# Rearranging the last image and the expert tiles of a hybrid conv-attention-MoE kernel

## The chip, the cores and the metric

The kernel runs on one core of a Trainium2 chip. The metric is the device time in microseconds of one execution, as the median of a few runs. A profile is one execution taken by the hardware profiler; its span goes from the first to the last instruction.

## The reference

Four images of 128 channels x 1024 positions pass through three blocks. (1) Attention over positions: `q, k` of 16 channels, `v` of 128, softmax over 1024 keys, `gamma * out + x`. (2) A linear attention without softmax over the tokens of `_ln_t(t)`: eight heads, whose scores reduce to one factor per head; then `@ proj_w + proj_b`, added to `t`. (3) A mixture of eight experts on `_ln_t(t)`, top 2 of 8:

```python
probs = softmax(flat @ router_w.T); topk_probs, topk_idx = top_k(probs, 2)
topk_probs = topk_probs / (sum(topk_probs) + 1e-09)
gates = einsum('nk,nke->ne', topk_probs, one_hot(topk_idx, 8))
h = silu(einsum('nc,ehc->neh', flat, w1)) * einsum('nc,ehc->neh', flat, w3)
out = einsum('ne,nec->nc', gates, einsum('neh,ech->nec', h, w2))   # t + out is returned
```

Each expert has 341 hidden channels. All is float32.

## The kernel before, in words

The program is a `Block` with one instruction stream per engine, written out by hand: SyncE (`sp`), TensorE (`pe`), ScalarE (`act`), VectorE (`dve`), GpSimd (`pool`). An engine runs its stream in order; semaphores join the streams. So the order of the calls in `image()` and in the tile loops is the schedule.

*Images.* For each of the four images the streams run `image(i)`: softmax attention (`weigh_values`), layer norm, then eight heads in turn (`head_values`: six matmuls of 512 columns; ScalarE keeps the high part in `keep_head_values`, L774; VectorE the low part in `low_head_values`, L960), each pair followed by `project_heads`. Beside it stand the scores of the next image (`beside(n)`: `scores_by_query` and `row_max`) and the routing of the image before: `shift_logits`, `pick_first`, `pick_second`, `keep_ranks` (rank of each token within its expert), `set_slots` (L1061 to L1064: row numbers in the table), and `set_gates` (L1040 to L1047: the two gates). `keep_outT` (L971) adds the bias to a half of the projection, `turn_out` (L507) turns it, `linear_attended` (L977 on) adds it to the token rows and takes statistics, `rstds` on GpSimd (L1323) gives the reciprocal deviation, `norm2` (L932) normalises.

*Row scatters.* GpSimd's `scatter_rows` writes the tokens' normalised rows to `xs_dram`, a table in DRAM with a region per expert: 16 indirect DMAs per image (2 choices x 8 tiles of 128 tokens), each row being 128 values, the result's row number and three spare words (528 bytes). For images 0 to 2 they go out during the next image, 12 ahead of the `rstd` of its second norm and 4 behind it (`SCATTERS_FIRST`).

*Expert tiles.* After the last image come 71 tiles of 128 rows, 41 from rows of images 0 to 2 (`early_table` gives their expert and first row, on one partition of VectorE) and 30 late ones (`late_counts`, `late_table`). For tile t: SyncE gathers 128 rows into one of 8 slots (L337, waits for the result scatter of tile t-8); TensorE turns them (`turn_x`, L622), ScalarE and VectorE split them in a high part (`high_part`, L829) and a low part (`low_part`, L1246); TensorE makes both hidden matrices (`hidden13`, six matmuls into `bank_s`, L372), ScalarE the silu (L824), VectorE the product (`multiply`, L1251); TensorE turns it (L643), VectorE keeps it (`keep_hiddenT`, L1256), TensorE makes the result, ScalarE copies it (`keep_y`, L835), GpSimd scatters it to `y_dram` (L1363). The weights `w13` are split beforehand in two halves (`split_w13`: ScalarE L751, VectorE L1069). The stages of neighbouring tiles overlap.

*Side jobs.* The second half of the last image's rows, its routing, its 16 row scatters (one after each result scatter of tiles 10 to 25) and 8 pad scatters (tiles 26 to 33, `place_pad`: rows of zeros behind each expert's last row) are done between tiles. Tile 41's gather waits for them all.

*Tail.* When all results are scattered, SyncE loads both choices of each of 8 half images (L362), VectorE does gate0 * y0 + t (L1299), ScalarE gate1 * y1 (L865), TensorE adds and turns both by matmuls with the identity, VectorE copies (L1305), SyncE stores (L365).

## Time and profile before

| | us |
|---|---|
| median of 3 runs (549.94 to 553.61) | 552.88 |
| profiled execution, its own time | 552.03 |
| its span | 550.1 |
| TensorE busy in the span | 460.2 (84%) |
| VectorE busy | 316.8 (58%) |
| ScalarE busy | 191.7 (35%) |
| GpSimd busy | 158.7 (29%) |
| mean granted TensorE clock | 0.901 |

Engines in the rows: PE is TensorE's matmuls, PEld its weight loads, DVE VectorE, ACT ScalarE, POOL GpSimd, SP SyncE. "L960" is line 960 of the kernel. A row of the timeline has start and length in us and, in brackets, the engine's idle time before it and what ended it ("remote" is a releaser that the profile doesn't tell). Buffers that share memory carry the name of the first: `probs_sb` is also the gathered rows, results and loads of the tail, `qk_sum_sb` the product, `w_rest_sb` the low part of `w13`.

### The profile page before, as it was taken

The numbers are of one execution on the slowest core, as the hardware profiler recorded it, in microseconds if no ns is written. First come the engines' busy times: TensorE is split into PE (matmuls) and PEld (weight loads), VectorE is DVE, ScalarE is ACT, GpSimd is POOL, SyncE is SP. The second block draws the span as 40 slices with busy tenths as digits, with TensorE's granted clock in tenths as the row PEclk, the third lists the DMA queues.
The fourth block names the chain that finished last, engine by engine and source line by source line (L and its number), as shares of the span: only waits on it lengthen the run. The fifth ranks groups of instructions, "written<-read, shape, count | busy, mean of one in ns | idle before, by whom it ended". The sixth has DMA issues, their size and how long they took to land.

```text
span 550.1 us, 9237 instructions
## 1 busy us (share of the span) xinstructions
PE 460.2 (84%) x2929; PEld 397.3 (72%) x2929; DVE 316.8 (58%) x871; ACT 191.7 (35%) x398; POOL 158.7 (29%) x168
## 2 busy tenths in 40 slices
PE   5879999998889988899875847987778689999847
PEld 3449667887657976578864646987677689999747
DVE  3854687467746569455647734656533345555436
ACT  3060534516217243134133403452222234444343
POOL 1000000100623202504107331335666554444500
PEclk9668999998969989879956986988998989999969
DMA  6800100001100002100001001212222222222187
GB/s 195 281 2 0 39 0 2 1 2 38 41 20 11 12 0 83 45 1 21 1 16 63 15 21 40 55 40 65 64 65 68 63 63 60 69 60 70 41 235 229
DMA packets 28869, 30.21 MB, mean 55 GB/s; under 512 B 5074, under 2 KB 24146, under 8 KB 28696
## 3 DMA queue, kind: packets, MB, share of 16 engines
q1 hardware_dynamic: 24248, 20.09, 13.1%
q0 software_dynamic: 4576, 9.53, 5.1%
q8 instruction: 27, 0.44, 0.3%
q14 instruction: 18, 0.15, 0.1%
HBM read 17.44 MB, written 12.16 MB: 54 GB/s over the span
## 4 chain that ended last, share of the span: by engine, by line
PE 61%; DVE 16%; issue 7%; another core or an unknown queue 5%; ACT 5%; DMA 3%; POOL 1%; SPq 1%; DVEq 0%; POOLq 0%; ACTq 0%
PE bank_c L372 25%; PE bank_s L372 19%; PE bank_a L372 9%; DVE row_max_sb L899 3%; PE bank_c L643 3%; DVE values_sb L960 3%; PE bank_a L622 1%; PE bank_c L443 1%; DVE v_ext_sb L892 1%; DMA probs_sb<-xs_dram 1%; ACT probs_sb L744 1%; DMA y_dram<-probs_sb 1%; DVE ln_sb L932 1%; PE bank_a L507 1%
## 5 line engine op out<-in xcount | busy, mean ns | idle before, releaser
L1363 POOL DMA_INDIRECT y_dram<-probs_sb x71 | 68.0, 957 | 83.8 <-ACT probs_sb L835 80.0
L1331 POOL DMA_INDIRECT xs_dram<-ln2x_sb,slots_sb x64 | 64.7, 1011 | 63.9 <-DVE slots_sb L1064 45.6
L1323 POOL TENSOR_TENSOR rstd_sb<-var_eps_sb,minus_half_sb 128x4 f32<-128x4 f32 x16 | 16.4, 1022 | 195.1 <-DVE var_eps_sb L926 195.1
L774 ACT ACTIVATE values_sb<-bank_s,g_head_sb 128x1024 fp32r<-128x1024 f32 x32 | 35.3, 1113 | 90.9 <-PE bank_s L372 59.7
L372 PE MATMUL bank_c<-v_ext_sb,probs_sb 128*128 128x129 f32 x512 | 62.5, 283 | 4.8 <-issue 3.5
L372 PEld LDWEIGHTS bank_c<-v_ext_sb,probs_sb 128*128 128x128 f32 x512 | 60.9, 198 | 6.7 <-issue 6.7
L372 PE MATMUL bank_c<-values_sb,wp_hi_sb 128*128 128x256 f32 x256 | 59.6, 310 | 0.0
L899 DVE TENSOR_REDUCE row_max_sb<-bank_a 128x1 f32<-128x512 f32 x64 | 41.5, 685 | 27.5 <-remote 14.3
L372 PE MATMUL bank_s<-probs_sb,x_hi_sb 128*128 x142 | 53.4, 376 | 2.9 <-issue 1.4
L372 PEld LDWEIGHTS bank_c<-values_sb,wp_hi_sb 128*128 128x128 f32 x256 | 46.9, 211 | 5.7 <-issue 4.7
L372 PE MATMUL bank_s<-probs_sb,x_lo_sb 128*128 x142 | 47.1, 331 | 0.0
L372 PE MATMUL bank_s<-w_rest_sb,x_hi_sb 128*128 x142 | 47.0, 331 | 0.0
L960 DVE SCALAR_TENSOR_TENSOR values_sb<-bank_s,g_head_sb,values_sb 128x1024 fp32r<-128x1024 f32 x32 | 40.5, 1277 | 7.5 <-ACT values_sb L774 7.4
L1251 DVE TENSOR_TENSOR qk_sum_sb<-probs_sb,bank_s 128x341 f32<-128x341 f32 x36 | 18.4, 512 | 41.8 <-ACT probs_sb L824 29.6
L835 ACT COPY probs_sb<-bank_c 128x128 f32<-128x128 f32 x71 | 18.9, 266 | 63.0 <-PE bank_c L372 35.8
L1256 DVE COPY qk_hi_sb<-bank_c 114x384 f32<-114x384 f32 x71 | 38.9, 548 | 2.9 <-remote 1.5
L1251 DVE TENSOR_TENSOR qk_sum_sb<-v_ext_sb,bank_s 128x341 f32<-128x341 f32 x35 | 17.8, 509 | 38.8 <-ACT v_ext_sb L824 36.9
L643 PE MATMUL bank_c<-cst_s_sb,qk_sum_sb 128*114 128x128 f32 x213 | 36.1, 280 | 3.9 <-DVE qk_hi_sb L1256 3.2
L372 PE MATMUL bank_c<-values_sb,wp_lo_sb 128*128 128x256 f32 x128 | 38.6, 302 | 0.0
L372 PE MATMUL bank_c<-wq_s_sb,qk_hi_sb 114*128 x142 | 29.4, 289 | 10.4 <-ACT probs_sb L835 10.4
L372 PE MATMUL bank_a<-k_stack_sb,q_stack_sb 64*128 64x512 f32 x64 | 31.0, 542 | 8.2 <-DVE row_max_sb L899 3.0
L744 ACT ACTIVATE probs_sb<-bank_s 128x1024 f32<-128x1024 f32 x32 | 32.3, 1024 | 9.2 <-PE bank_s L372 7.6
(189 smaller groups left out, 915.8 us busy)
## 6 DMA issues: line engine op xcount, KB each, us to landing
probs_sb<-xs_dram SPq DMA_DIRECT2D x71, 66.0 KB
probs_sb<-y_dram SPq DMA_DIRECT2D x16, 256.0 KB, 5.2
w_rest_sb<-in_w_dram SPq DMA_DIRECT2D x1, 2728.0 KB, 12.6
xc_sb<-in_x_dram SPq DMA_DIRECT2D x4, 512.0 KB, 3.3
y_dram<-probs_sb POOLq DMA_INDIRECT x71
xs_dram<-ln2x_sb,slots_sb POOLq DMA_INDIRECT x64
xs_dram<-pads_sb SPq DMA_DIRECT2D x1, 528.0 KB, 7.4
wq_s_sb<-in_wq_dram SPq DMA_DIRECT2D x1, 512.0 KB, 3.9
```

The lines of the kernel that those rows point to most:

```text
L372: return nc.tensor.matmul(bank, lhsT, rhs, start=start, stop=stop)
L643: last = nc.tensor.transpose(bank_c[0][0:CHUNK, c * P:(c + 1) * P], hidden[k % 2][:, c * CHUNK:(c + 1) * CHUNK], ident)
L744: nc.scalar.activation(probs[:, m, :], bank_s[m % 2][:, :], ACT.Exp, scale=DQK ** -0.5).then_inc(s.drained, 1)
L774: nc.scalar.activation(vh_hi[:, hd % RING, :], bank_s[hd % 2][:, :], ACT.Copy, scale=g_head[:, hd:hd + 1]).then_inc(vh_high, 1)
L835: nc.scalar.copy(y_rows[k], bank_c[1][:, 0:C]).then_inc(y_kept, 1)
L899: V.reduce_max(row_max2[:, n, h:h + 1], bank_a[h][:, :], AX_X).then_inc(A[h].drained, 1)
L960: V.scalar_tensor_tensor(out=vh_lo[:, hd % RING, :], in0=bank_s[hd % 2][:, :], scalar=g_head[:, hd:hd + 1], in1=vh_hi[:, hd % RING, :].bit ...
L1251: V.tensor_tensor(hidden[k % 2][:, 0:HID], silu1[k % 2], bank_s[k % 2][:, H13 + HID:H13 + HID2], ALU.mult).then_inc(hidden_ready, 1)
L1256: V.tensor_copy(hiddenT[k % 2][0:CHUNK], bank_c[0][0:CHUNK, 0:3 * P].rearrange("p (k n) -> p k n", n=P)).then_inc(hiddenT_ready, 1)
L1323: G.tensor_tensor(rstd[:, tiles], var_eps[:, tiles], minus_half[:, tiles], ALU.pow).then_inc(rstd_ready, 1)
L1331: G.indirect_dma_start(xs_dram, bass.IndirectOffsetOnAxis(ap=slots[:, i, k:k + 1], axis=0), ln2x[:, k // TILES, k % TILES, :], None).then_ ...
L1363: G.indirect_dma_start(y_dram, bass.IndirectOffsetOnAxis(ap=x_rows[k][:, C:C + 1].bitcast(I32), axis=0), y_rows[k], None).then_inc(scatter ...
```

## The change

It rearranges the last image, the tiles and the tail. In all images the gates are made right behind the slots, and travel to the table inside the row (word C+1); the result is scaled by its gate when ScalarE keeps it, and the tail adds only. The order of the results in `y_dram` becomes 8 rows in line for each partition, so the tail's loads take 2048 bytes in line instead of 512.

- *VectorE, image i:* `set_slots(i-1)` and now `set_gates(i-1)` behind low part 0. In the last image both stand ahead of `head_weights`; `early_table` moves from behind low part 0 to behind low part 3; `split_w13(0)` behind `keep_outT(i, 0)`, which itself comes before low parts 6 and 7; then `low_part(0)`, `split_w13(1)`, `low_part(1)`, `linear_attended(i, 0)`, `keep_outT(i, 1)`. `norm2(last, 0)` moves behind tile 0.
- *GpSimd:* all 16 row scatters of image 2 ahead of the `rstd` (they now wait for the gates). Row scatters of the last image from tile 9, behind two tiles of three. The 8 pad scatters go.
- *SyncE:* the pads are 8 plain DMAs, behind the gather of tile 23, from registers with the first row number.
- *TensorE:* `turn_out(last, 0)` behind the seventh head; the first two `turn_x` inside the last projection; routing of the last image at tiles 2, 3 and 6 instead of 4, 5 and 10. In the tail 4 transposes per half instead of 8 matmuls of code.
- *VectorE, tiles:* routing steps packed.

```diff
+    ROWS_FROM = 9
+    PADS_AT = 20
...
+            def place_pads():
+                sp.wait_ge(pads_placed, 1)
+                for e in range(0, EXPERTS, 4):
+                    rows = nc.values_load_multi_w_load_instructions(pad_rows[0:1, e:e + 4], engines=[mybir.EngineType.SP], min_val=0,
+                                                                    max_val=EXPERTS * REGION - P)[1]
+                    for n in range(4):
+                        sp.dma_start(xs_dram[bass.ds(rows[n], P), :], pads[:, e + n, :]).then_inc(pads_stored, 16)
...
+                    if half == 0 and j == PADS_AT:
+                        place_pads()
...
-                    rows = y_dram[k * TOKENS + h * HALF:k * TOKENS + (h + 1) * HALF, :]
-                    sp.dma_start(y_in[:, h, k], rows.rearrange("(n p) c -> p n c", p=P)).then_inc(y_loaded[h], 16)
+                    rows = y_dram[k * TOKENS + h // 2 * N:k * TOKENS + (h // 2 + 1) * N, :].rearrange("(p n) c -> p n c", p=P)
+                    sp.dma_start(y_in[:, h, k], rows[:, h % 2 * 4:h % 2 * 4 + 4, :]).then_inc(y_loaded[h][k], 16)
...
+                if last:
+                    turn_out(i, 0)
...
-                    if k == 1:
+                    if k == 1 and not last:
                         turn_out(i, 0)
+                    if last and k in (4, 7):
+                        turn_x(k // 7, k // 7)
...
-                if t == 4:
+                if t == 2:
                     turn_ln2(final, 1)
-                if t == 5:
+                if t == 3:
                     for h in range(2):
                         route(final, h)
-                if t == 10:
+                if t == 6:
                     rank(final)
...
-                    for k in range(2):
-                        last = mm(bank_a[h % 2][:, j * P:(j + 1) * P], y_in[:, h, k, j, :], ident, start=(k == 0), stop=(k == 1))
+                    last = nc.tensor.transpose(bank_a[h % 2][:, j * P:(j + 1) * P], y_in[:, h, 0, j, :], ident)
...
-                    if i == IMAGES - 1 and hd in (1, 4):
+                    if i == IMAGES - 1 and hd in (3, 5):
                         split_w13(slice(4 * (hd // 4) * HID2, 4 * (hd // 4 + 1) * HID2))
...
-                nc.scalar.copy(y_rows[k], bank_c[1][:, 0:C]).then_inc(y_kept, 1)
+                nc.scalar.activation(y_rows[k], bank_c[1][:, 0:C], ACT.Copy, scale=x_rows[k][:, C + 1:C + 2]).then_inc(y_kept, 1)
...
-                act.wait_ge(y_loaded[h], 32)
-                for j in range(4):
-                    last = nc.scalar.activation(y_in[:, h, 1, j, :], y_in[:, h, 1, j, :], ACT.Copy, scale=gates[:, 1, 4 * h + j:4 * h + j + 1])
-                last.then_inc(y_scaled, 1)
+                act.wait_ge(y_turned, h + 1)
+                nc.scalar.copy(y_out[h], bank_a[h % 2][:, :]).then_inc(out_kept, 1)
...
-                g = [gates[:, k, bass.ds(i * TILES, TILES)] for k in range(2)]
+                g = [ln2x[:, k, :, C + 1] for k in range(2)]
...
                 low_lnT(i)
-                if not last:
+                if last:
+                    set_slots(i - 1)
+                    set_gates(i - 1)
+                    V.memset(hidden[0][:, HID:3 * CHUNK], 0.0)
+                    V.memset(hidden[1][:, HID:3 * CHUNK], 0.0).then_inc(hidden_cleared, 1)
+                else:
                     make_stacks(i + 1)
                 head_weights(i)
...
-                if not first:
+                if not first and not last:
                     set_slots(i - 1)
-                if last:
-                    early_table()
+                    set_gates(i - 1)
...
                 low_head_values(i, 3)
+                keep_bias(i)
                 if last:
-                    split_w13(0)
-                keep_bias(i)
+                    early_table()
...
+                if last:
+                    keep_outT(i, 0)
+                    split_w13(0)
+                else:
                     negate_max(i + 1)
                 low_head_values(i, 6)
+                low_head_values(i, 7)
                 if last:
+                    low_part(0, 0)
                     split_w13(1)
-                low_head_values(i, 7)
-                keep_outT(i, 0)
-                linear_attended(i, 0)
-                if not first and not last:
-                    set_gates(i - 1)
-                keep_outT(i, 1)
-                norm2(i, 0)
+                    low_part(1, 1)
+                    linear_attended(i, 0)
+                    keep_outT(i, 1)
+                else:
+                    keep_outT(i, 0)
+                    linear_attended(i, 0)
+                    keep_outT(i, 1)
+                    norm2(i, 0)
...
                 if t == 0:
+                    norm2(last, 0)
                     linear_attended(last, 1)
-                if t == 2:
+                if t == 1:
                     norm2(last, 1)
+                if t == 3:
+                    shift_logits(last)
                 if t == 4:
-                    set_gates(last - 1)
+                    pick_first(last)
                 if t == 5:
-                    shift_logits(last)
-                if t == 6:
-                    pick_first(last)
-                if t == 8:
                     pick_second(last)
-                if t == 10:
+                if t == 7:
                     keep_ranks(last)
                     place_pads()
+                    set_slots(last)
+                if t == 8:
+                    set_gates(last)
+                if t == 9:
+                    late_counts()
                 if t == 11:
-                    set_slots(last)
-                if t == 13:
-                    late_counts()
-                if t == 15:
                     late_table()
-                if t == 18:
-                    set_gates(last)
...
+            def add_up(h):
+                for k, other in enumerate((t2[:, 4 * h:4 * h + 4, :], y_in[:, h, 1])):
+                    dve.wait_ge(y_loaded[h][k], 16)
+                    V.tensor_tensor(y_in[:, h, 0], y_in[:, h, 0], other, ALU.add).then_inc(y_added, 1)
...
-                if 10 <= t < 26:
-                    scatter_rows(last, range(t - 10, t - 9))
-                if t == 26:
-                    pool.wait_ge(pads_placed, 1)
-                if 26 <= t < 34:
-                    place_pad(t - 26)
+                if ROWS_FROM <= t and (t - ROWS_FROM) % 3 < 2 and (t - ROWS_FROM) // 3 < TILES:
+                    k = (t - ROWS_FROM) // 3 * 2 + (t - ROWS_FROM) % 3
+                    scatter_rows(last, range(k, k + 1))
```

## Rows read from the trace of the kernel before

**Rows 1.** Windows: us, then busy us and count per engine, granted clock, DMA, GB/s.

```profile
core 0: us, PE busy (x) PEld busy (x) DVE busy (x) ACT busy (x) POOL busy (x), PEclk, DMA share, GB/s
...
314.00:334.50 20.50, 7.36 (x43) 6.59 (x42) 8.34 (x23) 1.06 (x3) 4.95 (x5) 0.77 0.10 28
...
386.00:441.00 55.00, 41.07 (x279) 37.22 (x278) 21.94 (x60) 14.45 (x52) 32.83 (x35) 0.97 0.25 65
...
529.70:550.10 20.40, 17.03 (x128) 16.30 (x128) 12.96 (x36) 8.95 (x28) 0.00 (x0) 0.91 0.87 252
```

**Rows 2.** Timeline of VectorE in the last image, 285 to 329 us.

```profile
285.92 0.17 DVE L945 TENSOR_REDUCE qsum_sb<-bank_c 128x8 f32<-128x16 f32 x1 [5.21 <-PE bank_c L372]
...
289.58 0.18 DVE L1064 CAST slots_sb<-small_sb 128x16 int32<-128x16 f32 x1
...
295.99 2.48 DVE L960 SCALAR_TENSOR_TENSOR values_sb<-bank_s,g_head_sb,values_sb 128x1024 fp32r<-128x1024 f32 x2
...
302.64 2.99 DVE L1069 TENSOR_TENSOR w_rest_sb<-w_rest_sb,probs_sb 128x2728 fp32r<-128x2728 f32 x1
...
328.23 0.18 DVE L990 TENSOR_SCALAR ln2x_sb<-tok_sb 128x16 int32<-128x16 int32 x1 [3.27 <-DMA xs_dram<-ln2x_sb,slots_sb]
```

**Rows 3.** Timeline of GpSimd in the last image: first, eleventh and last row scatter.

```profile
290.05 1.03 POOL L1331 DMA_INDIRECT xs_dram<-ln2x_sb,slots_sb  x1 [14.12 <-DVE slots_sb L1064]
...
302.76 3.71 POOL L1331 DMA_INDIRECT xs_dram<-ln2x_sb,slots_sb  x1 [0.30 <-issue]
...
325.94 0.95 POOL L1331 DMA_INDIRECT xs_dram<-ln2x_sb,slots_sb  x1 [0.30 <-issue]
```

**Rows 4.** Timeline of TensorE in the last image, up to the first turned rows.

```profile
297.33 1.22 PE L372 MATMUL bank_s<-lnT_hi_sb,wv_hi_sb 128*128 128x512 f32 x2 [5.61 <-DVE values_sb L960]
...
332.05 0.45 PE L622 MATMUL bank_a<-cst_s_sb,probs_sb 128*128 128x128 f32 x1 [7.82 <-DMA probs_sb<-xs_dram]
```

**Rows 5.** Chain of waits: the six matmuls of tile 0 and of a late tile.

```profile
334.55 2.07 PE bank_s L372 x6
...
514.41 0.94 PE bank_s L372 x6
```

**Rows 6.** Timeline of VectorE: products of tiles 0, 11, 37, 70, and the first gate step.

```profile
337.14 0.51 DVE L1251 TENSOR_TENSOR qk_sum_sb<-probs_sb,bank_s 128x341 f32<-128x341 f32 x1 [2.87 <-ACT probs_sb L824]
...
347.00 0.21 DVE L1040 TENSOR_REDUCE small_sb<-prob_sb 128x8 f32<-128x64 f32 x1
...
367.14 0.51 DVE L1251 TENSOR_TENSOR qk_sum_sb<-v_ext_sb,bank_s 128x341 f32<-128x341 f32 x1 [1.05 <-ACT v_ext_sb L824]
...
447.50 0.51 DVE L1251 TENSOR_TENSOR qk_sum_sb<-v_ext_sb,bank_s 128x341 f32<-128x341 f32 x1 [1.50 <-ACT v_ext_sb L824]
...
517.82 0.51 DVE L1251 TENSOR_TENSOR qk_sum_sb<-probs_sb,bank_s 128x341 f32<-128x341 f32 x1 [0.97 <-ACT probs_sb L824]
```

**Rows 7.** Timeline of GpSimd: two pairs of tiles with extra scatters, and a late tile.

```profile
403.21 0.96 POOL L1363 DMA_INDIRECT y_dram<-probs_sb  x1 [1.60 <-ACT probs_sb L835]
404.47 0.95 POOL L1331 DMA_INDIRECT xs_dram<-ln2x_sb,slots_sb  x1 [0.30 <-issue]
...
409.52 0.95 POOL L1363 DMA_INDIRECT y_dram<-probs_sb  x1 [1.57 <-ACT probs_sb L835]
...
512.94 0.95 POOL L1363 DMA_INDIRECT y_dram<-probs_sb  x1 [1.10 <-ACT probs_sb L835]
```

**Rows 8.** Timeline of VectorE: set-up into image 0, and image 2.

```profile
43.48 0.17 DVE L915 RECIPROCAL rden_sb<-bank_c 128x1 f32<-128x1 f32 x1 [8.78 <-PE bank_c L372]
...
228.63 1.41 DVE L899 TENSOR_REDUCE row_max_sb<-bank_a 128x1 f32<-128x512 f32 x2 [5.72 <-remote]
```

**Rows 9.** DMA view of the tail: GB/s in 40 slices, first 532 to 538 us, then 539 to 543.

```profile
GB/s 307 300 294 297 304 290 280 304 283 290 294 294 280 304 287 280 304 290 280 290 304 280 277 311 280 287 300 287 283 304 287 283 290 300 277 300 297 280 283 307
...
GB/s 297 282 312 261 323 282 313 307 323 369 389 333 338 476 446 369 328 471 430 410 328 430 430 430 328 410 451 451 328 348 512 369 307 225 266 205 123 82 266 389
```

**Rows 10.** The kept result by group, and the tail's timeline: first scaling, last copy.

```profile
L835 ACT COPY probs_sb<-bank_c 128x128 f32<-128x128 f32 x71 | 18.9, 266 | 63.0 <-PE bank_c L372 35.8 <-remote 22.7 <-issue 4.5
...
528.32 1.28 ACT L865 ACTIVATE probs_sb<-probs_sb,gates_sb 128x128 f32<-128x128 f32 x4 [6.42 <-DMA probs_sb<-y_dram]
...
546.95 0.69 DVE L1305 COPY xt_sb<-bank_a 128x512 f32<-128x512 f32 x1 [1.09 <-PE bank_a L372]
```

More of the change, by code:

```diff
@@ L171, in conv_attn_moe_kernel @@
         both = sb("both", [P, TILES, EXPERTS], BF16)
-        gates = sb("gates", [P, 2, IMAGES * TILES])
+        place8 = sb("place8", [P, 1])
         base = sb("base", [P, EXPERTS])
@@ L537, in rank, with turn_x @@
                 last.then_inc(uses.filled, 1)
+            def turn_x(t, k):
+                if t == 0:
+                    pe.wait_ge(A[1].drained, A[1].after(IMAGES - 2, "ln2", 1))
+                at_least(pe, x_lo_ready, t)
+                pe.wait_ge(gathered[k], gathered_value(t, k))
+                nc.tensor.transpose(bank_a[1][:, 0:P], x_rows[k][:, 0:C], ident).then_inc(x_turned, 1)
             def image(i, first=False, last=False):
@@ L785, in copy_ln2, with high_part @@
                 nc.scalar.copy(ln2x[:, 1, 4 * h:4 * h + 4, 0:C], ln2x[:, 0, 4 * h:4 * h + 4, 0:C]).then_inc(ln2_copied, 1)
+            def high_part(t, k):
+                act.wait_ge(x_turned, t + 1)
+                at_least(act, h13_ready, t - 1)
+                nc.scalar.copy(x_hi[k % 2][:], bank_a[1][:, 0:P]).then_inc(x_hi_ready, 1)
             def gate_exps(i):
@@ L852, in _ @@
                     copy_ln2(last, 0)
-                if t == 4:
+                if t == 2:
                     keep_ln2T(last, 1)
                     copy_ln2(last, 1)
-                if t == 8:
+                if t == 5:
                     gate_exps(last)
@@ L1339, in image @@
                     rstds(i, which)
+                early = 2 * TILES if i == IMAGES - 1 else SCATTERS_FIRST
                 if not first:
-                    scatter_rows(i - 1, range(SCATTERS_FIRST))
+                    scatter_rows(i - 1, range(early))
                 rstds(i, 2)
-                if not first:
-                    scatter_rows(i - 1, range(SCATTERS_FIRST, 2 * TILES))
+                if not first and i < IMAGES - 1:
+                    scatter_rows(i - 1, range(early, 2 * TILES))
                 if i < IMAGES - 1:
```

65 lines of the change are left out of this document (18 added, 47 removed).

## Prediction

> **What bounds the kernel now.** I read first the busy time by stretch [rows 1]: after the last image come three stages that wait. From 314 to 334.5 us TensorE is busy 7.36 of 20.5 us; from 386 to 441 it is busy 41.07 of 55, GpSimd 32.83; from 529.7 on the DMA engines are busy 87% of the time. The images before are only brushed by the change.
>
> Then the timelines around the start of the expert tiles [rows 2 to 4]. VectorE waits 5.21 us for the column sums, makes the slots of image 2 at 289.58 and then runs the early table up to 295.99, for which TensorE waits 5.61 us. GpSimd starts the 16 row scatters at 290.05; they follow by 1.26 us each (0.96 and a gap of 0.30); the eleventh takes 3.71. The queue then stops for a reciprocal deviation of the last image, and the last scatter starts at 325.94. VectorE, which waits for them all, goes on at 328.23; TensorE turns the first gathered rows at 332.05, after 7.82 us of waiting, and starts tile 0 at 334.55 [rows 5]. The start hangs on GpSimd's last scatter, not on TensorE.
>
> Then the tiles. The products of tiles 0, 11, 37 and 70 start at 337.14, 367.14, 447.50 and 517.82 [rows 6]. An undisturbed tile takes 2.05 us (scatter 0.95, wait 1.10). Where a row or pad scatter follows each result scatter (24 tiles, 10 to 33), GpSimd issues four in a row, and the next pair of tiles begins 6.31 us later (403.21, 409.52): 3.16 per tile [rows 7]. GpSimd alone would allow 2 x 1.26 = 2.52; the rest is a wait for a result that TensorE hands over late. I see the same lateness in image 2: VectorE stands 5.72 us amid a chain of twelve scatters [rows 8]. In the tail, loads of 512-byte rows run near 290 GB/s; once stores of 2048-byte rows take over, the slices lie around 390 [rows 9]. The 8 halves take 2.4 us each (first scaling 528.32, last copy ends at 547.64 [rows 10]).
>
> **Part by part, in the profiled execution (552.03 us, span 550.1; 0.85 under the median of 552.88).**
>
> *Images 1 and 2: +3.3 us.* The eight gate operations move ahead of the second low part of the heads. They take 1.65 us (the first takes 0.21 [rows 6]; eight such). VectorE is on the path there, so it costs that in each of two images; where they stood, VectorE waits for TensorE afterwards, and nothing comes back. Least 0, if the lateness swallows it; most 3.5. Three small operations added in the set-up lie before VectorE's wait of 8.78 us [rows 8]: 0, uncovered 0.5.
>
> *Start of the tiles: -14 us.* Slots and gates of image 2 go ahead of the head weights, into the 5.21 us wait: 0.95 + 1.65 us from 280.7 on, so scatters start at 283.6. All 16 now stand ahead of the reciprocal deviation: last issue 302.6, landed at 304.8 (325.94 to 328.23 was 2.3). The early table (6.2 us) stands behind the fourth low part. Walking VectorE's new order (low part 1.28, half 0.7): fourth low part done 296.8, table 303.2, fifth and sixth low parts 305.8, out half 306.5, first split 309.5, last two low parts 312.1. The gather needs table and scatters (304.8) and 3.8 us more (328.23 to 332.05 before): 308.6, and the first rows are turned inside the last projection at 312.8. Behind it VectorE has low part 0 (0.3), the second split (2.99), low part 1, the first half's sum and statistics (2.1) and an out half (0.7): first product at 320, 17 us under 337.14. The stretch now runs beside unbroken scatters, as image 2 does; I charge 3 of its 5.72 us: 323. Bounds: -17 (no lateness) and -8 (5.72 and a wait like it again).
>
> The eleventh scatter's 3.71 us begin 0.12 us behind VectorE's split of 2.99 us [rows 2, 3]. The Trainium skill ("SBUF — State Buffer", Who interferes with whom) says that a VectorE operation with two SBUF inputs holds off a GpSimd operation that reads SBUF; the trace agrees. By that rule the split, now at 306.5, meets no scatter; the walk has it so without the rule.
>
> *Tiles 0 to 11: +4 us.* Before: 30.0 us, 7.5 over 11 x 2.05. The same side jobs stay, closer together; slots (0.8), late counts (1.9) and the first half's normalisation (1.1) come in, gates replace gates. 34 us. Bounds 30 and 38 (the late table's 3.3 too).
>
> *Tiles 11 to 32.* Row scatters follow two tiles of three, from 9 to 31; the pads leave GpSimd. Three tiles are five instructions: 5 x 1.26 = 6.3 us, against 6.15 of undisturbed tiles. If the extra 1.27 us (6.31 less 4 x 1.26) is paid once per group, three tiles take 7.6 us, 2.5 each, which I take. Floor 2.1 (GpSimd's pace), ceiling 3.16 (nothing eased). 21 x 2.5 + 2 for the late table = 54.5 us.
>
> Pads on SyncE: two loads of four registers and 8 transfers of 67 KB, ahead of the gather of tile 24. At 290 GB/s they are 1.9 us of DMA; the issues are not shown by rows here, I take 0.5 us each. Gathers run 8 tiles ahead, so this comes to 0; most 3 once.
>
> *Tiles 32 to 70:* 38 x 2.13 ((517.82 - 447.50) / 33) = 80.9. Scaling in ScalarE's copy of the result costs about 0.05 us (1.28 for four scaled ones, 0.266 for a copy [rows 10]), covered by ScalarE's idle time; uncovered 0.05 x 71 = 4. Product 0 to product 70: 34 + 54.5 + 80.9 = 169.4 against 180.7: -11.3.
>
> *Tail: -6.5 us.* Up to 526, where loads begin to move, nothing changes. They now take 2048-byte rows: 4.19 MB at 390 instead of 290 GB/s, 10.8 against 14.5 us; the stores (2.1 MB, 5.4 us) stand behind them: 526 + 16.2 + 1.3 to land = 543.5. Beside that, per half: VectorE two sums of 512 columns (0.6 each, from 2.99 us for 2728), TensorE 4 transposes in place of 16 matmuls (128 for 8 halves [rows 1]), ScalarE one copy (at most the 0.69 of VectorE's [rows 10]): 1.35 us per half, last copy at 539.7. DMA sets the end. Bounds -1 (below) and -8.
>
> The page "DMA: Bandwidth & Descriptors" of the Trainium skill (Specifications) puts the least transfer for line rate at 512 B; by that larger rows bring nothing, a rival below.
>
> **Sum:** 3.3 - 14 - 11.3 - 6.5 = -28.5; span 521.6, time 523.5, by the median 524.4. I say 524.
>
> **Rivals.** (a) *The lateness does not ease.* Tiles 11 to 32 stay at 3.16, because GpSimd has hardly a gap left: 21 x 0.66 = +14: 538. Against: four instructions per two tiles become 3.3. (b) *It goes*, GpSimd is merely full: 21 x 0.4 = -8: 516. (c) *The last image is held by its own scatters* in full: +6: 530. For: image 2; against: image 3 had scatters from 290 and its long waits were for VectorE [rows 4]. (d) *Larger rows load no faster*: 6.29 MB at 290 GB/s are 21.7 us from 526, then 1.3: 549 in place of 543.5: 529.5. The fast slices are mostly stores. (e) *Slower: the clock.* The granted clock was 0.77 in the stretch 314 to 334.5 and 0.97 in 386 to 441 [rows 1]. If VectorE's lumps, now packed into tiles 0 to 11, and the bursts behind them hold it at 1.2 GHz up to tile 32, a tile costs 3.7 us (tile 0's six matmuls took 2.07 us, first load included, a late tile's 0.94 [rows 5]; I take 1.8 times 2.05): 33 x 3.7 = 122 against 88.5: +34, 558. It decides from some 28 such tiles on. Against: 14 us of idling in 55 left the clock at 0.97. (f) *The change does not do what it says*: with 40 instructions end to end the row scatters and pads end no sooner. Same time as (a), in its chance.
>
> **Chances.** Forecast (518 to 529) 0.40; (a) 0.17; (b) 0.20; (c) 0.11; (d) 0.09; (e) 0.03. Range 510 to 538: it takes in (b), (c), (d) and most of (a); what is left out is where two of them fall together, (a)'s far side and (e), some 0.2. A measurement of this kernel tells about 1% from no change: faster by over 1% (under 547.4) 0.95, within 0.02, slower 0.03 with (e).
>
> **What would show it.** Row scatters of image 2 start near 284 and are unbroken; first product near 323 (wrong from 331 on). Tiles 11 to 32 in 50 to 58 us, in groups of five GpSimd instructions and then a wait near 1.6 us; no such wait means (b), over 64 us (a). Loads near 390 GB/s in the tail, last copy within 15 us of the first load's start. The granted clock over 0.9 from tile 2 on. The forecast is wrong if the first product comes at 331 or later, or the end stays 28 us behind the last scatter.

## The result, and the profile after

The changed kernel takes 534.8 us (median of 4 runs, 530.93 to 540.41) against 553.25 for the kernel before, a ratio of 0.971 (95% interval 0.965 to 0.977). The profiled execution took 533.97 us with a span of 532.2 and a granted clock of 0.889, so 17.9 us of span are gone. The longest of the four (540.41) is a slow run and is left out of the ratio. I had forecast 524, within a range of 510 to 538: the direction was right, the size was not, and the two terms that missed most are the images and tiles 11 to 32.

The images first. These are the reciprocal deviations behind the row scatters of images 1 and 2, in GpSimd's timeline of the kernel before:

```profile
173.48 1.04 POOL L1323 TENSOR_TENSOR rstd_sb<-var_eps_sb,minus_half_sb 128x4 f32<-128x4 f32 x1 [18.01 <-DVE var_eps_sb L926]
...
249.35 1.04 POOL L1323 TENSOR_TENSOR rstd_sb<-var_eps_sb,minus_half_sb 128x4 f32<-128x4 f32 x1 [18.66 <-DVE var_eps_sb L926]
```

and of the changed kernel, with the first row scatter of the last image:

```profile
173.40 1.04 POOL L1332 TENSOR_TENSOR rstd_sb<-var_eps_sb,minus_half_sb 128x4 f32<-128x4 f32 x1 [15.76 <-DVE var_eps_sb L936]
...
249.33 1.04 POOL L1332 TENSOR_TENSOR rstd_sb<-var_eps_sb,minus_half_sb 128x4 f32<-128x4 f32 x1 [16.98 <-DVE var_eps_sb L936]
...
283.11 1.03 POOL L1340 DMA_INDIRECT xs_dram<-ln2x_sb,slots_sb  x1 [7.23 <-DVE ln2x_sb L1057]
```

The gate operations that moved ahead in images 1 and 2 cost nothing; GpSimd waits less by what it starts later. The scatters of image 2 start at 283.11 (290.05 before, [rows 3]) and run unbroken; the last starts at 302.12. VectorE's timeline in the last image (it answers to [rows 2] and the first of [rows 6]):

```profile
300.94 0.20 DVE L1108 SCALAR_TENSOR_TENSOR expert_f_sb<-expert_f_sb,cst_s_sb 1x48 f32<-1x48 f32 x1 [0.41 <-DVE rows_sb L1107]
302.35 0.19 DVE L1110 TENSOR_REDUCE word_f_sb<-expert_f_sb 1x6 f32<-1x48 f32 x1 [1.20 <-DVE expert_f_sb L1108]
...
304.48 0.16 DVE L1121 TENSOR_SCALAR taken_sb<-taken_sb 1x8 f32<-1x8 f32 x1 [1.18 <-DVE taken_sb L1120]
...
324.07 0.51 DVE L1272 TENSOR_TENSOR qk_sum_sb<-probs_sb,bank_s 128x341 f32<-128x341 f32 x1 [0.64 <-ACT probs_sb L841]
```

Here the lateness is seen at work (that an engine goes on well after what it waits for is done): VectorE waits 1.2 us for its own last operation (0.2 us of work on one partition), once while scatters are being issued and once up to 304.48, 1.4 us after the last of them has been issued. In the window 298 to 306, TensorE is busy 2.34 of 8 us and ScalarE not at all:

```profile
298.00:306.00 8.00, 2.34 (x11) 1.91 (x10) 3.19 (x12) 0.00 (x0) 3.85 (x5) 0.73 0.13 42
```

The first product comes at 324.07, 13.1 us earlier than before. The products of tiles 11, 32, 37 and 70 in the changed kernel:

```profile
355.15 0.50 DVE L1272 TENSOR_TENSOR qk_sum_sb<-v_ext_sb,bank_s 128x341 f32<-128x341 f32 x1
...
421.99 0.51 DVE L1272 TENSOR_TENSOR qk_sum_sb<-probs_sb,bank_s 128x341 f32<-128x341 f32 x1 [1.42 <-ACT probs_sb L841]
...
434.96 0.51 DVE L1272 TENSOR_TENSOR qk_sum_sb<-v_ext_sb,bank_s 128x341 f32<-128x341 f32 x1 [0.88 <-ACT v_ext_sb L841]
...
504.70 0.51 DVE L1272 TENSOR_TENSOR qk_sum_sb<-probs_sb,bank_s 128x341 f32<-128x341 f32 x1 [0.96 <-ACT probs_sb L841]
```

From product 0 to product 70 are 180.6 us, as before (180.7, [rows 6]): the whole stage, for which I had forecast 11.3 us less, gained nothing. Products 11 to 32 take 66.8 us, and one place stands out. SyncE's queue in the changed kernel:

```profile
379.68 6.93 SPq L347 DMA_DIRECT2D xs_dram<-pads_sb  x8
389.25 1.93 SPq L339 DMA_DIRECT2D probs_sb<-xs_dram  x4
```

TensorE's timeline, the turning of tile 24's rows:

```profile
391.30 0.45 PE L556 MATMUL bank_a<-cst_s_sb,probs_sb 128*128 128x128 f32 x1 [5.42 <-DMA probs_sb<-xs_dram]
```

And the windows around it (us, busy us and count of PE, PEld, DVE, ACT, POOL, granted clock, DMA, GB/s):

```profile
386.00:388.00 2.00, 0.00 (x0) 0.00 (x0) 0.11 (x1) 0.46 (x1) 1.52 (x2) 1.00 0.35 105
388.00:390.00 2.00, 0.00 (x0) 0.00 (x0) 0.40 (x1) 0.00 (x0) 0.00 (x0) 1.00 0.11 38
390.00:392.00 2.00, 0.70 (x4) 0.73 (x5) 0.00 (x0) 0.22 (x1) 0.00 (x0) 0.61 0.50 109
392.00:394.00 2.00, 2.00 (x10) 2.00 (x9) 0.85 (x2) 0.34 (x2) 0.00 (x0) 0.50 0.09 26
394.00:396.00 2.00, 2.00 (x9) 1.94 (x9) 0.10 (x1) 0.66 (x3) 0.96 (x1) 0.50 0.08 29
```

The pads stand ahead of the gathers of tiles 24 to 27; TensorE idles 5.42 us, and then works 5 us at half clock (1.2 of 2.4 GHz). Here the stall is paid a second time behind it.

The tail: last result scatter, loads and ScalarE's last copy, from the timelines of GpSimd, SyncE and ScalarE:

```profile
509.27 0.96 POOL L1370 DMA_INDIRECT y_dram<-probs_sb  x1 [0.62 <-ACT probs_sb L847]
...
511.67 8.42 SPq L374 DMA_DIRECT2D probs_sb<-y_dram  x16
...
528.79 0.58 ACT L876 COPY xt_sb<-bank_a 128x512 f32<-128x512 f32 x1 [0.74 <-PE bank_a L724]
```

The DMA view of 508 to 533, GB/s in 40 slices of 0.63 us (it answers to [rows 9]):

```profile
GB/s 7 39 66 0 105 0 0 105 272 328 347 275 220 147 174 246 275 397 390 410 400 400 403 416 380 397 387 393 403 413 403 403 400 390 347 249 292 20 0 0
```

From product 70 to the end are 27.5 us instead of 32.3. The 2048-byte rows do load at 380 to 416 GB/s (added up from 512.4 us on, the slices reach the 4.19 MB of the loads near 525.5), but not from the start: in the first 5.6 us of the load the slices lie between 147 and 347.

### The profile page after: what moved, and what is told of

The parts are those of the page before. It is cut to its first block, busy times and chain, and to the rows that moved or that the text cites. A ratio compares the mean times of both kernels' runs of the same rounds, so it can differ in the third digit from the quotient of the medians.

```text
span 532.2 us, 9038 instructions
## 1 busy us (share of the span) xinstructions
PE 451.4 (85%) x2833; PEld 386.0 (73%) x2833; DVE 313.3 (59%) x850; ACT 194.6 (37%) x374; POOL 148.2 (28%) x160
## 4 chain that ended last, share of the span: by engine, by line
PE 58%; DVE 18%; issue 9%; ACT 5%; another core or an unknown queue 3%; DMA 3%; SPq 3%; POOL 0%; DVEq 0%; POOLq 0%; ACTq 0%
PE bank_c L384 25%; PE bank_s L384 18%; PE bank_a L384 7%; PE bank_c L659 4%; DVE row_max_sb L909 3%; DVE values_sb L970 2%; DVE probs_sb L1315 1%; DVE qk_hi_sb L1277 1%; DMA probs_sb<-y_dram 1%; DVE w_rest_sb L1079 1%; DMA y_dram<-probs_sb 1%; PE bank_a L556 1%; DVE v_ext_sb L902 1%; ACT probs_sb L756 1%
## 5 line engine op out<-in xcount | busy, mean ns | idle before, releaser
L1340 POOL DMA_INDIRECT xs_dram<-ln2x_sb,slots_sb x64 | 61.8, 966 | 60.6 <-DVE ln2x_sb L1057 42.2
L384 PE MATMUL bank_s<-probs_sb,x_hi_sb 128*128 x142 | 53.3, 375 | 3.4 <-issue 2.9
L909 DVE TENSOR_REDUCE row_max_sb<-bank_a 128x1 f32<-128x512 f32 x64 | 41.3, 686 | 24.1 <-PE bank_a L384 18.3
L847 ACT ACTIVATE probs_sb<-bank_c,probs_sb 128x128 f32<-128x128 f32 x71 | 26.1, 368 | 50.0 <-PE bank_c L384 43.7
L1272 DVE TENSOR_TENSOR qk_sum_sb<-v_ext_sb,bank_s 128x341 f32<-128x341 f32 x35 | 17.8, 508 | 30.7 <-ACT v_ext_sb L841 26.1
L659 PEld LDWEIGHTS bank_c<-cst_s_sb,qk_sum_sb 128*114 128x114 f32 x213 | 25.5, 140 | 9.3 <-issue 7.3
```

The source lines that it names most:

```text
L384: return nc.tensor.matmul(bank, lhsT, rhs, start=start, stop=stop)
L659: last = nc.tensor.transpose(bank_c[0][0:CHUNK, c * P:(c + 1) * P], hidden[k % 2][:, c * CHUNK:(c + 1) * CHUNK], ident)
L847: nc.scalar.activation(y_rows[k], bank_c[1][:, 0:C], ACT.Copy, scale=x_rows[k][:, C + 1:C + 2]).then_inc(y_kept, 1)
L909: V.reduce_max(row_max2[:, n, h:h + 1], bank_a[h][:, :], AX_X).then_inc(A[h].drained, 1)
L1272: V.tensor_tensor(hidden[k % 2][:, 0:HID], silu1[k % 2], bank_s[k % 2][:, H13 + HID:H13 + HID2], ALU.mult).then_inc(hidden_ready, 1)
L1340: G.indirect_dma_start(xs_dram, bass.IndirectOffsetOnAxis(ap=slots[:, i, k:k + 1], axis=0), ln2x[:, k // TILES, k % TILES, :], None).then_ ...
```

## Experiments

All ratios are to the kernel before, run on the same chip; the text quoted is what was on record before the run. "e1" and so on stand for the labels.

**e1_pads_spread.** From tile 16 on, SyncE does one piece of the pads' work behind each gather.

```diff
-                    if half == 0 and j == PADS_AT:
-                        place_pads()
+                        if half == 0 and j + n >= PADS_AT - 4:
+                            next(pad_jobs, None)
```

(`place_pads` yields behind its loads of four registers and behind each pad.)

> The changed kernel, but the eight pads on SyncE go one behind each gather from tile 16's on instead of in one block ahead of the gather of tile 24. Theory: the block (register loads 2.8 us, eight issues 6.93 us) made gather 24 late, TensorE waited 5.42 us for it, and the clock fell behind that: products 19 to 24 took 20.5 us; now about 15 (5 x 2.95), everything after comes 5 to 6 us earlier: span about 527 in place of 532.2, ratio about 0.96. Rival: SyncE's loads of registers between the gathers make several gathers late in place of one: 19 to 24 still 19 us or more, span 531 or more.

Measured: 527.1 us (525.3 to 529.0), ratio 0.962 (0.954 to 0.971); span 526.3. Products 19 to 24: 379.15 to 393.87, 14.7 us. Product 0 to 70: 173.4 us. The theory holds: the block cost 180.6 - 173.4 = 7.2 us, of which the idling was 5.4; that the half clock behind it is the rest is read from the windows, not tested. One trace against one says this only roughly: eight runs have this order of tiles (e1, e4 to e8, e10, e11), and products 19 to 24 take 12.7 to 14.7 us in all of them, against 20.5 in the changed kernel, but products 11 to 37 range from 72.9 to 77.2.

**e2_rows_every_tile, e3_rows_one_in_two, e12_pads_on_gpsimd.** The price of one more scatter on GpSimd, in three rhythms.

```diff
-                if ROWS_FROM <= t and (t - ROWS_FROM) % 3 < 2 and (t - ROWS_FROM) // 3 < TILES:
+                if ROWS_FROM <= t < ROWS_FROM + 2 * TILES:                    # e2
+                after_tile = [*range(ROWS_FROM, 26, 2), *range(27, 34)]       # e3
+                if t in after_tile:
```

e12 is e2 with GpSimd scattering pad t - 25 behind tiles 25 to 32, through a column of slots as in the kernel before, and SyncE placing none.

> As e1_pads_spread, but one row scatter behind each result scatter of tiles 9 to 24, as in the kernel before. Theory A (each additional scatter costs the same whatever the rhythm, (3 x 2.91 - 6.15) / 2 = 1.3 us): products 11 to 24 at 3.35 us a tile, 25 to 32 at 2.1, product 32 within 1 us of e1_pads_spread. Theory B (the extra wait is paid once per group of four instructions on GpSimd, the kernel before had 3.16 a tile): 3.16 a tile, product 32 about 2.5 us earlier than in e1_pads_spread. Rival C (the denser rhythm is what costs, as I thought when I took 2.5 for two in three): 3.6 or more a tile, product 32 some 4 us later.

> As e1_pads_spread, but row scatters behind tiles 9, 11, ... 25 (one in two) and then 27 to 33 (each tile): two rhythms in one run. Theory A (1.3 us for each additional scatter): products 11 to 25 at 2.7 us a tile, 27 to 33 at 3.35. Theory B (GpSimd's own pace decides: 3 x 1.26 = 3.8 us of issues fit into two undisturbed tiles of 4.1): 2.05 to 2.2 a tile from 11 to 25, and 3.16 from 27 to 33; product 34 about 5 us earlier than under A.

> As e2_rows_every_tile, but the eight pads are scattered by GpSimd behind tiles 25 to 32, one each, instead of being stored by SyncE between the gathers. Theory A (a further scatter costs 1.2 us for each, whatever it is and wherever it stands): product 37 about 9 us later against product 11 than in e2_rows_every_tile (72.4 us there, 81 to 82 here), median near 536. Rival B (GpSimd has room for one further scatter in a tile while nothing else is pressed): under 4 us later, median 528 to 531.

Measured: e2 527.6 us, ratio 0.967 (0.957 to 0.978); e3 526.3 us, 0.962 (0.954 to 0.971); e12 537.4 us, 0.972 (0.966 to 0.977). Products 11 and 37, from VectorE's timeline, first of e2, then of e12:

```profile
356.38 0.50 DVE L1276 TENSOR_TENSOR qk_sum_sb<-v_ext_sb,bank_s 128x341 f32<-128x341 f32 x1
...
428.79 0.51 DVE L1276 TENSOR_TENSOR qk_sum_sb<-v_ext_sb,bank_s 128x341 f32<-128x341 f32 x1 [0.88 <-issue]
```

```profile
356.34 0.50 DVE L1263 TENSOR_TENSOR qk_sum_sb<-v_ext_sb,bank_s 128x341 f32<-128x341 f32 x1
...
438.36 0.51 DVE L1263 TENSOR_TENSOR qk_sum_sb<-v_ext_sb,bank_s 128x341 f32<-128x341 f32 x1 [1.23 <-issue]
```

Eight more scatters cost 82.0 - 72.4 = 9.6 us, 1.2 each, as theory A has it for e12 (81 to 82; rival B had under 4 us more). As executions of one order of tiles differ by up to 4.4 us here, this is 5 to 10 us, and it is the price of a pad on GpSimd less that on SyncE. 26 undisturbed tiles are 53.3 us; e2's 16 scatters and the late table therefore cost 19.1, e1's (two in three tiles) 19.7, the 24 of the kernel before 27.1.

The finer forecasts fit less well. In e2 products 11 to 24 take 3.13 us a tile, which is theory B's 3.16 and not A's 3.35, but product 32 comes 3.0 us later than in e1 (A: within 1; B: 2.5 earlier; C: 4 later). In e3 products 11 to 25 take 36.18 us, 2.58 a tile, between A's 2.7 and B's 2.05 to 2.2; from 27 to 33 it is 2.70, under both (3.35 and 3.16). The late table lies behind product 11 in all of them. From product 13 to 25, past it, a tile takes 2.44 us in e3, 2.71 in e1 and 3.03 in e2, against 2.05 undisturbed: 0.8, 1.0 and 1.0 us for each scatter. So A holds in the main, with a smaller price than its 1.3 us and a lower one still where scatters are sparse; that GpSimd's own pace decides (B) falls in e3, where its three instructions (3.8 us) left it idle for 1.5 us in every pair of tiles and the pair still took 5.05. None of e1, e2 and e3 is clear of the others by its ratio.

**e9_rows_after_landing.** e3, with a wait ahead of the row scatters of tiles 9 to 25.

```diff
+                    if t < 26:
+                        pool.wait_ge(scattered[t % SLOTS8], scattered_value(t, t % SLOTS8))
```

> As e3_rows_one_in_two, but in the stretch with one row scatter in two tiles (9 to 25) the row scatter waits until the result scatter ahead of it has landed, so that the two are not in flight together. In e3_rows_one_in_two products 11 to 25 took 36.18 us (2.58 a tile). Theory O (what a further scatter costs comes from two scatters in flight one upon the other, as in the bursts of the images): 2.1 to 2.3 a tile, product 25 4 to 6 us earlier relative to product 11. Rival P (the price belongs to each scatter, in whatever company; the wait now adds about 1 us before the next result scatter): 2.6 or more a tile.

Measured: 529.5 us, ratio 0.961 (0.955 to 0.966); products 11 to 25 at 354.22 and 391.82, 2.69 a tile. The number is the rival's, but the run doesn't decide. GpSimd's timeline:

```profile
371.45 0.96 POOL L1344 DMA_INDIRECT xs_dram<-ln2x_sb,slots_sb  x1 [1.55 <-DMA y_dram<-probs_sb]
372.71 0.96 POOL L1374 DMA_INDIRECT y_dram<-probs_sb  x1 [0.30 <-issue]
373.98 0.96 POOL L1374 DMA_INDIRECT y_dram<-probs_sb  x1 [0.31 <-issue]
376.49 0.96 POOL L1344 DMA_INDIRECT xs_dram<-ln2x_sb,slots_sb  x1 [1.55 <-DMA y_dram<-probs_sb]
```

From 366 us on every pair of tiles takes the same 5.03 us (wait for landing, three scatters, two gaps), with no wait for a result. The wait that I put in has filled GpSimd, and would hide what theory O forecasts. Why a scatter costs about 1 us although no engine is full stays open; I did not separate TensorE's and ScalarE's handshakes from it.

**e4_bursts_of_four, e8_bursts_of_two.** Gaps in the bursts of the images.

```diff
                 for k in ks:
+                    if i < last and k % 4 == 0 and k > ks[0]:
+                        pool.wait_ge(xs_stored[i], 16 * k)
```

(e8: `k % 2`.)

> As e1_pads_spread, but the 16 row scatters of images 0 to 2 wait after each four until all of these have landed: gaps of about 2 us in a burst that ran unbroken at 1.26 us. Theory L (signals of TensorE and VectorE come late only in long unbroken bursts, from some 9 us in): the long waits beside the bursts go: in the last image VectorE's fifth low part comes near 303 instead of 307.35, the last row scatter lands near 310, first product 1 to 3 us earlier, and images 1 and 2 each end 1 to 3 us earlier: span 3 to 8 us under e1_pads_spread. Rival M (the lateness is paid for each scatter in flight, however spaced): images 1 and 2 unchanged or later by up to 3 us, and in the last image the gathers wait for the later end (landed 310 instead of 304.8): first product 2 to 5 us later.

> As e4_bursts_of_four, but the row scatters of images 0 to 2 wait for landing after every second. Theory L2 (what remained in e4_bursts_of_four, waits of 4 us in the last image, is still lateness, and shorter bursts take it away): images 1 and 2 end another 1 to 3 us earlier, span 515 to 518. Rival E (bursts of four had taken away what there was; 16 scatters now take 16 x 2.1 = 33 us and end later): images unchanged, the row scatters of image 2 land near 312 in the last image and the first product comes 1 to 4 us later than 318.27, span 520 to 524.

Measured: e4 522.5 us (521.2 to 524.7), ratio 0.955 (0.947 to 0.964); all four of its runs lie under all four of e1 on the same chip. e8 532.0 us, ratio 0.970 (0.964 to 0.975). Windows in image 2, of the kernel before, whose burst began at 215.78:

```profile
224.00:226.00 2.00, 2.00 (x8) 1.15 (x7) 0.00 (x0) 0.00 (x0) 1.39 (x3) 1.00 0.10 34
226.00:228.00 2.00, 0.68 (x3) 0.20 (x2) 0.00 (x0) 0.09 (x1) 1.69 (x2) 1.00 0.20 68
228.00:230.00 2.00, 0.62 (x1) 0.18 (x1) 1.34 (x3) 1.03 (x1) 1.39 (x3) 0.88 0.10 34
230.00:232.00 2.00, 1.96 (x7) 1.47 (x7) 1.23 (x2) 0.00 (x0) 0.69 (x1) 0.50 0.20 68
...
236.00:238.00 2.00, 2.00 (x11) 1.90 (x10) 0.63 (x2) 0.00 (x0) 0.00 (x0) 0.50 0.00 0
```

and of e4, whose first burst began at 216.49:

```profile
224.00:226.00 2.00, 2.00 (x8) 1.14 (x8) 0.39 (x1) 0.81 (x1) 1.54 (x2) 1.00 0.20 68
226.00:228.00 2.00, 2.00 (x9) 1.10 (x8) 2.00 (x3) 0.87 (x2) 1.33 (x2) 1.00 0.10 34
...
232.00:234.00 2.00, 2.00 (x9) 1.14 (x8) 0.24 (x1) 0.66 (x1) 1.68 (x2) 1.00 0.20 68
```

In the unbroken burst of the kernel before, TensorE, VectorE and ScalarE all but stand still from 226 to 228.6 (TensorE to 229.4), and TensorE then runs at half clock until nearly 240; in bursts of four it works through at full clock. From the first scatter to the reciprocal deviation, image 2 takes 26.1 us, 32.2 in e1; image 1 takes 29.0 against 30.8.

But not all of the 6 us of image 2 belong to the gaps. This is e1, whose unbroken burst of image 2 began at 217.50:

```profile
219.00:221.00 2.00, 2.00 (x7) 1.18 (x6) 1.92 (x3) 0.26 (x1) 1.70 (x2) 0.64 0.20 68
221.00:223.00 2.00, 2.00 (x7) 1.35 (x7) 1.54 (x3) 0.85 (x1) 1.39 (x3) 0.50 0.18 61
...
229.00:231.00 2.00, 2.00 (x8) 1.34 (x8) 0.86 (x2) 0.90 (x1) 1.70 (x2) 1.00 0.20 68
```

TensorE does not stand still in it, and the clock fell at 219 to 221, before the place of e4's first gap. So bursts must be compared at like clocks. These are the times from the first scatter to the reciprocal deviation in images 1 and 2 of all kernels but the one before:

| granted clock | unbroken bursts | bursts with gaps |
|---|---|---|
| full before, fell in the first 5 us | 30.7 to 32.4 (twelve: changed kernel, e1, e2, e5, e6, e7, e9, e12) | 29.0 to 29.1 (e4, e8, e11) |
| full in the first 5 us | 30.0 (e5) | 26.1 (e4) |
| half before and for 12 us more | 31.8 to 33.3 (e2, e3, e7, e12) | 31.8, 31.8 (e10) |
| half before, rose in the first 5 us | 33.8 (e3) | 27.4, 27.4 (e8, e11) |

By these single traces gaps are worth 0 to 1.5 us at half clock, otherwise 2 to 6. What decides over the clock stays open: just before, TensorE was as idle in e4 (busy 0.43 of 2 us from 216) as in e1 (0.42 from 217), and only e1's clock fell.

In the last image nothing came: 41.6 us from the first scatter to the first product, 41.3 in e1. There the end of the scatters binds again (first gather at 308.58, 9.7 us ahead of the product), and in e8 more so (gather 316.39, 47.2 us): theory L2 falls, and rival E holds, though e8's first product came 7.7 us later than e4's, and not 1 to 4. That gaps shorten images 1 and 2 holds; that this is because TensorE no longer stands still is shown only where it did (226 to 229 above). In the last image theory L fell: the gaps cost what they freed.

**e10_last_in_sixes, e11_last_in_eights.** Fours in images 0 and 1; in the last image, a gap after every sixth, or after the eighth.

```diff
-                    if i < last and k % 4 == 0 and k > ks[0]:
+                    if i < last and k % (6 if i == last - 1 else 4) == 0 and k > ks[0]:
```

> As e4_bursts_of_four, but in the last image the row scatters of image 2 wait for landing after every sixth, not after every fourth (images 0 and 1 keep their fours). In e4_bursts_of_four the last image's scatters start at 276.65, the first gather goes out at 308.58 and the first product is at 318.27. Theory G (there the end of the scatters binds again: gather to first product is 9.7 us, against 18 in e1_pads_spread): scatters land near 301, first gather at 303 or earlier, VectorE's walk binds: first product at 313 to 315, span 515 to 517. Rival L6 (a burst of six is long enough to make signals late): gather early, but VectorE or ScalarE wait 3 us and more between 285 and 300, first product at 318 or later.

> As e10_last_in_sixes, but the last image's 16 row scatters wait for landing once, after the eighth. In e10_last_in_sixes the first product came 37.7 us after the first of these scatters, the first gather 28.7 after it; in e1_pads_spread (unbroken) 41.3 and 23.2. Theory G (the end of the scatters binds while the bursts are short): one gap of 1.7 us less, first gather 27 us after the first scatter, first product 36 to 37 after it; median 519 to 522. Rival L8 (eight in a row are long enough for TensorE to stand still): TensorE idles 3 us or more between the seventh and the tenth scatter's landing, first product 39 to 41 after the first scatter; median 523 to 526.

Measured: e10 522.0 us (520.4 to 527.2), ratio 0.945 (0.940 to 0.949), the fastest of all against the kernel before, clear of the changed kernel's 0.971 but not of e4's 0.955 (0.947 to 0.964); e11 524.4 us, 0.952 (0.947 to 0.957). From the first scatter of the last image to the first product: 37.7 us in e10, 38.3 in e11. The latter lies between its two theories (36 to 37, and 39 to 41). In e11 TensorE is busy 0.66 of 2 us from 294 and 0.68 from 298, then at half clock, and VectorE 0.48 of 2 us from 296. e4 and e10 have one such gap of TensorE each (0.84 from 295, 0.66 from 300), but with VectorE busy throughout; one trace hints that eight are too many, and the ratios of e10 and e11 don't tell them apart. In e10 the first product came at 321.51, not at 313 to 315 as theory G has it, because its last image began at 283.84, 7.2 us later than e4's; counted from there, 37.7 us is what G gives (36.4 to 38.4). The first gather was 2.3 us later than G's, and GpSimd's timeline says why:

```profile
303.15 3.66 POOL L1346 DMA_INDIRECT xs_dram<-ln2x_sb,slots_sb  x1 [0.30 <-issue]
```

This scatter fell beside VectorE's split again (303.00 to 305.99), which costs 2.7 us more, with the gathers (312.51) waiting behind it. It is the eleventh scatter of [rows 3] once more, and the change had moved the scatters clear of it. The Trainium skill ("SBUF — State Buffer", Who interferes with whom) has a VectorE instruction with two SBUF inputs contend with a GpSimd instruction that reads SBUF; these traces agree.

The profiled execution of e10 took 527.2 us, the longest of its four, and shows what bursts don't explain. Windows of image 2, whose burst began at 217.97:

```profile
209.00:211.00 2.00, 2.00 (x17) 1.94 (x17) 1.61 (x4) 0.00 (x0) 0.00 (x0) 1.00 0.36 143
211.00:213.00 2.00, 2.00 (x6) 1.13 (x5) 1.93 (x6) 1.50 (x2) 0.00 (x0) 0.61 0.39 160
...
229.00:231.00 2.00, 2.00 (x8) 1.79 (x8) 0.00 (x0) 0.00 (x0) 0.42 (x2) 0.50 0.10 34
```

TensorE had half clock from 212 to 231 with no stop like the one above. The clock fell ahead of the burst, and image 2 took 75.1 us from reciprocal deviation to reciprocal deviation (e4 71.4, the kernel before 75.9). Which executions get this I can't say. Single executions of e10 differ by up to 7 us, and the longest has the lowest mean clock (0.893, against 0.903 to 0.915), so the verdict on the bursts rests on the medians.

**e5_rows_turned_late, e6_slots_later.** What made the start early.

```diff
# e5: both turns and both low parts behind the last projection again
-                    if last and k in (4, 7):
-                        turn_x(k // 7, k // 7)
# e6: in the last image too, slots and gates behind the first low part
-                    set_slots(i - 1)
-                    set_gates(i - 1)
```

> As e1_pads_spread, but the first two tiles' rows are turned and split behind the last projection again, as in the kernel before. By the walk: VectorE's last out half ends at 324.05 there, both low parts then stand in front of TensorE's six matmuls (1.5 us) and ScalarE's silu (0.45 us): first product near 327, 1.5 to 2 us later than 325.10, and the span with it (528). Rival: the turning was never in anyone's way, since VectorE's work up to 324 sets the first product: within 0.5 us.

> As e1_pads_spread, but in the last image slots and gates of image 2 are made behind the first low part of the heads, as in the kernel before: row scatters start near 292 instead of 283.83, the last lands near 313, first gathers near 316. Theory S (in the changed kernel the scatters end 10 us before their rows are turned, so their end no longer sets the start; what sets it is VectorE's own row of work): first product within 2.5 us of 325.10. Rival (the prediction's reading carried on: the start hangs on the last row scatter): 6 us or more later, 331 or more.

Measured: e5 528.6 us, ratio 0.965 (0.957 to 0.974); e6 532.0 us, 0.970 (0.964 to 0.975). First products at 326.60 and 329.02. e5's last image itself began 0.7 us later than e1's, so the turning is worth 0.8 to 1.5 us, under the 1.5 to 2 of its theory and over its rival's 0.5; by the ratio e5 is not clear of e1. e6's first product comes 3.9 us later than e1's, between the two theories. Its windows (the scatters start from 291.86 to 311.05):

```profile
306.00:308.00 2.00, 0.36 (x2) 0.00 (x0) 0.13 (x1) 1.27 (x2) 1.69 (x2) 1.00 0.20 68
308.00:310.00 2.00, 0.00 (x0) 0.00 (x0) 1.16 (x1) 2.00 (x1) 1.39 (x3) 1.00 0.10 34
310.00:312.00 2.00, 0.00 (x0) 0.00 (x0) 0.00 (x0) 0.19 (x1) 1.70 (x2) 0.85 0.21 68
312.00:314.00 2.00, 0.00 (x0) 0.00 (x0) 0.00 (x0) 0.00 (x0) 0.01 (x1) 0.50 0.10 34
```

TensorE stands still here too until the last scatter has landed, and VectorE and ScalarE end only what they have at hand (one low part; one value and one cast of `w13`'s second half). In each of the nine unbroken bursts of sixteen (the changed kernel, e1, e2, e3, e5, e6, e7, e9, e12) TensorE is busy 0 to 1 of every 2 us from the 16th to the 22nd us. Starting the burst 8 us later moves the stop behind more of the image's own work, and so 8 us of start are worth 3.9 us at the first product.

**e7_tail_rows_512.** The new tail on results stored in token order (VectorE makes the row numbers `tok` as in the kernel before, too).

```diff
-                    rows = y_dram[k * TOKENS + h // 2 * N:k * TOKENS + (h // 2 + 1) * N, :].rearrange("(p n) c -> p n c", p=P)
+                    rows = y_dram[k * TOKENS + h * HALF:k * TOKENS + (h + 1) * HALF, :].rearrange("(n p) c -> p n c", p=P)
```

> As e1_pads_spread, but the results are stored in token order again, so that the last loads fetch 512-byte rows, with everything else of the new tail (sums of whole halves, transposes, copies by ScalarE). From the last result scatter to the end of the span e1_pads_spread has 23.3 us. Theory (row size sets the load rate: 290 against 390 GB/s, 14.5 against 10.8 us): 3 to 4 us longer, 26.3 to 27.3. Rival (d) of the prediction (larger rows load no faster, the gain came from the engines' shorter steps): within 1 us of 23.3.

Measured: 532.2 us, ratio 0.968 (0.959 to 0.976); from the last result scatter (504.81) to the end 24.6 us. The DMA view of 503 to 530:

```profile
GB/s 30 0 103 0 36 61 0 22 205 329 316 260 280 266 255 316 332 322 291 297 288 300 292 291 290 291 290 288 296 375 398 410 407 404 404 358 355 109 0 0
```

and of the kernel before, 520 to 550.1:

```profile
GB/s 104 5 38 49 44 44 0 112 321 274 282 296 303 314 306 310 296 291 291 289 292 290 289 292 289 292 347 407 397 332 291 114 103 245 22 182 166 41 308 0
```

Both expectations miss: the larger rows are worth 1.3 us (e1: 23.3), neither 3 to 4 nor nothing, by one trace each. The rate is as the theory has it, 290 against 400 GB/s, but only over the second half of the load; in its first 6 us the small rows are no slower (205 to 332, against 131 to 383 in e1). The larger part of the tail's gain, 27.9 - 24.6 = 3.3 us, is the engines' shorter steps: DMA is now busy in every slice up to the last copy, where the old tail left slices between 22 and 308 GB/s over its last 6 us. The Trainium skill ("DMA: Bandwidth & Descriptors", Specifications) puts the least transfer for line rate at 512 B; by this trace 512-byte rows from DRAM get, in that second half, 0.73 of what 2048-byte rows get.

## Why the forecast was right, and where it was not

The span came out 10.6 us over my 521.6. That this lies within the range is in part luck: tiles 11 to 32 alone missed by 12.3 us, and two terms that I had put too high (images, 3.3; tiles 0 to 11, 2.9) gave back 6.2 of it. Step by step:

- *Images 1 and 2, +3.3:* 0, its lower bound. The step "VectorE is on the path there" failed: in 142 to 174 TensorE is busy 29.8 of 32 us, at a granted clock of 0.84, and VectorE waits for it (2.03 and 3.83 us inside the burst). The bound was named, the value was taken from the wrong end. The three small operations in the set-up, which I had put at 0, are seen at the first reciprocal deviation (98.56, 98.14 before), and are gone by image 1.
- *Start, -14:* -13.1, with the mechanism as put. Scatters at 283.1 (283.6 forecast), fourth low part done at 295.7 (296.8), first rows turned at 316.7 (312.8), first product at 324.07 (323). The lateness was 4 us, where I charged 3. What I had wrong is what the first product hangs on: not GpSimd's last scatter alone (8 us of its start are worth 3.9, e6) but VectorE's own work and the burst's stop as well.
- *Tiles 0 to 11, 34:* 31.1, inside the bounds.
- *Tiles 11 to 32, 54.5:* 66.8, over the ceiling of 3.16 a tile. Two steps failed. "The extra 1.27 us is paid once per group": 0.8 to 1.2 us are paid for each scatter (e2, e3, e12), which makes 60.2 in e1. And the pads, "this comes to 0; most 3 once", came to 7: I measured them against eight tiles of lead, but a gather has only what is left behind the scatter that frees its buffer. Tile 16's scatter went out at 377.64, tile 24's rows were wanted at 391.30 - 5.42 = 385.9, and between these fell the loads of registers and 6.93 us of issues, which I had put at 4 us; the half clock behind the stall I left out. Taking the pads off GpSimd was worth some 9.6 us (e12), and placing them in one block gave some 7 of these back (e1).
- *Tiles 32 to 70, 80.9:* 82.7; the first four tiles still ran beside the last scatters. Scaling in the copy is hidden, as forecast: products 37 to 70 take 69.7 us, 70.3 before [rows 6].
- *Tail, -6.5:* -4.8. Rate right; "DMA sets the end" holds from 6 us in. The start of the load was mis-sized, and the engines' part was the larger one (3.3 us; the rows 1.3, where I had 3.7).

Rival (a), 538, came nearest to the tiles, but by luck: its 3.16 us a tile are the measured 66.8 only with the stall at the pads in it; without it (e1) a tile takes 2.87, between (a) and my 2.5. Its reason is wrong, too: GpSimd had gaps, and they don't help. Rival (b) falls with it. Rival (d) fell on the rate, but for the larger rows its outcome (no gain) was nearer to 1.3 us than my 3.7. Rival (e) did not occur as a state of the stage, but in pieces of 5 to 10 us behind a stop. Of the signs that I had named, the start of the scatters, the first product, the rate of the loads and the granted clock (0.95 from 330 to 504) came as forecast; tiles 11 to 32 (66.8, not 50 to 58) did not, nor did the last copy, which ends 17.7 us after the first load's start, not 15.

## What to carry to other kernels

Spread work that is moved to another queue over the gaps between what it delays: here one block (6.93 us of issues and its loads of registers) cost 7.2 us, 5.42 of idling and the rest with a half clock behind it, and spread out no such stall is seen in eight runs. Price an indirect scatter by the piece (here 0.8 to 1.2 us), not by the free time of the engine that issues it. Try a wait for landing after every four to six scatters of a long run (here 522.5 us against 527.1), not after every two (532.0). And before an image's gain is put down to such a change, compare the granted clock of the two traces.
